# Layer 0 of a two-layer graph network on one core: where TensorE does a node group's values, turns and tables within its step

## The chip, the cores and the metric

The kernel runs on one core of one Trainium2 chip. The metric is the device time of one execution in microseconds (us); the time of a kernel is the median of several executions. Engines are named as in the profile: PE is TensorE, PEld its weight loads, DVE is VectorE, ACT is ScalarE, POOL is GpSimd, SP is SyncE, which here only issues DMAs.

## The reference

A graph of 6250 nodes (128 values each) and 200000 edges, sorted by destination node, passes through two layers, each followed by a residual sum and a layer norm.

```
# layer 0, a transformer convolution
h = x @ Wx.T + bx;  q, k, v = h @ Wq.T + bq, h @ Wk.T + bk, h @ Wv.T + bv
e = concat([msg, cos(|last_update[src] - t| * time_w + time_b)]) @ We.T
alpha = softmax over the edges of one dst of  sum(q[dst] * (k[src] + e)) / sqrt(128)
m = segment_sum((v[src] + e) * alpha, dst)
h = h + tanh(h @ A.T + m + b_ac);   x1 = layernorm(x + tanh(h))
# layer 1, an edge network: relu(concat(x1[src], x1[dst]) @ We1 + be1) @ We2 + be2,
# summed by dst, then a node network, residual and layer norm
```

## The kernel before

Layer 0 works on 196 chunks of 1024 edges (128 partitions by J = 8). Since the edges are sorted by destination, a chunk's destinations lie in a window of W = 80 nodes. The chunks are run by hardware loops: a turn of the loop holds 7 steps (SLOTS), u = 0 to 6, one chunk each, and there are 28 turns. Every engine runs its own list of steps, and the engines meet through semaphores. SLOTS = 7 is also the number of buffers for gathered rows (`he`).

What a step does for the chunks near c, engine by engine:

- POOL, `gather(c)` (L955 to L968): 8 indirect DMAs that fetch the rows of `h_table` for the chunk's sources into `he[u]`. Before them it waits for `sum_full`, that is, for TensorE's sums of the chunk that had this buffer seven chunks ago. TensorE sums chunk c-2 in its step c, so POOL starts the gathers of chunk c+5 when TensorE's sums in step c are reported.
- TensorE, `step(c)` (L1038): `spread_top` of chunk c-1 (L1014, to `p_small`), `turn_top(c)` (L1007), `scores` of c+1 (L989: 24 records of matmuls, as the profile counts them), `turn_back` of c-3 (L1031, 2 records), `sums` of c-2 (L1020, 16 records of 193 columns), and `turn` of c+2 (L971, 12 transposes: 4 for `turn_full[2]` and twice 4 for `turn_full[0]` and `[1]`).
- ACT: `copy_turns` of c+1 (L1131, three copies of `p_turn` to `heT`, in the order 2, 0, 1, each waiting for its `turn_full`), `copy_sums` of c-3 (L1123), then the sine features of c+2, exponentials of c-1, and the widened features of c+2.
- DVE: the phases of c+2, `tops_of_nodes(c)` (L1297, waits for `turn_top`), `diagonals`, `add` of c-4 (L1345), `fades` of c-3, `belows` of c-1, then `others` and `masks` of c+1 (L1281: two halves, each waiting for its half of the scores, and a reduction).

TensorE's `scores` of c+1 wait for ACT's three copies; its `turn_back` waits for `copy_sums` of c-3 and for DVE's `add` of c-4.

The last 13 turns (of 28, in a loop of 12 and one behind it) run `step_grouped` instead. They also take one group of 512 finished nodes (G) each through the end of layer 0 and make layer 1's tables of it. The stages are spread over the steps of a turn:

- u = 0: ACT copies the group's sums out of `acc` (`node_take`).
- u = 1: TensorE's `node_values` (L697, 24 records of matmuls into `p_turn[0]` to `[2]`, `val_full`), then DVE's `node_pre` (L715) behind its own step. The same `p_turn` buffers are wanted by `turn`, so TensorE waits for `pre_done` before `turn`.
- u = 2 to 4: tanh, layer norm (ACT and DVE).
- u = 5: TensorE's `node_turn` (L783, 4 transposes, `x1_full`), ACT's `node_copy_x1` (L789); TensorE waits for `x1T_done` before `turn`.
- u = 6: TensorE's `node_tables` (L796, 8 records of 256 columns, `tables_full`), DVE's `node_copy_rows` (L803) behind its own step; TensorE waits for `rows_done` before `turn`. ACT then stores the two tables.

Layer 1 is not touched: it has loops of its own, from L1684 on.

Of the kernel before, what the change touches and what calls it, by code (L numbers as in the profile page):

```python
# [38 lines left out]
def gnn_kernel(nc, x, src, dst, edge_attr, edge_weight, node_vec, time_w, time_b, Wx, bx, Wq, bq, Wk, bk,  # L39
# [28 lines left out]
    with ExitStack() as whole:  # L68
# [6 lines left out]
        def val(eng, v):  # L75
            return v if isinstance(v, int) else eng.snap(v)

        def again(eng, s, v):

            if not isinstance(v, int) or v > 0:  # L80
                eng.wait_ge(s, v)
# [393 lines left out]
        def shift(c, k):  # L475

            return c[0] + (c[1] + k) // SLOTS, (c[1] + k) % SLOTS
# [4 lines left out]
        def is_last(c):  # L482
            return isinstance(c[0], int) and number(c) == NCH - 1

        def is_first(c):
            return isinstance(c[0], int) and number(c) == 0
# [29 lines left out]
        with ExitStack() as ctx:  # L516
# [316 lines left out]
            def layer0_round(r):  # L833
# [3 lines left out]
                with ExitStack() as c2:  # L837
                    block = c2.enter_context(nc.Block())

                    def count(c):  # L840

                        return (c[0] + base) * SLOTS + c[1]
# [4 lines left out]
                    def prob_of(c):  # L847
                        return probs[third(c)]
# [10 lines left out]
                    def behind(c, k):  # L859

                        return not (isinstance(c[0], int) and number(c) < k)
# [108 lines left out]
                    def _(e):  # L970
                        def turn(c):  # L971

                            u = c[1]
                            n = count(c)
                            n0, n1 = val(e, n), val(e, n + 1)
                            e.wait_ge(he_done, n1)

                            again(e, turn_done[2], n0)
                            for k in range(J // 2):

                                mm = e.transpose(p_turn[2][:, k * P:(k + 1) * P], rest_of(c)[:, k, :, :].rearrange("p f q -> p (f q)"), ident[:, :])  # L981
                            mm.then_inc(turn_full[2], 1)
                            for h in range(2):
                                again(e, turn_done[h], n0)
                                for k in range(4):
                                    mm = e.transpose(p_turn[h][:, k * P:(k + 1) * P], he[u][:, 4 * h + k, A2:WIDE], ident[:, :])  # L986
                                mm.then_inc(turn_full[h], 1)

                        def scores(c):  # L989

                            u = c[1]
                            n = count(c)
                            n0, n1 = val(e, n), val(e, n + 1)
                            e.wait_ge(win_in[u], val(e, (c[0] + base) * 64 + 64))
                            e.wait_ge(turn_done[2], n1)
                            for h in range(2):
                                e.wait_ge(turn_done[h], n1)

                                again(e, masked[h], n0)
                                for k in (0, 2):  # L1000
                                    pair = (4 * h + k) // 2
                                    e.matmul(p_score[h][:, k:k + 2, :], heT2[:, pair * P:(pair + 1) * P], qk_two[u][:, :, :], start=True, stop=False)  # L1002
                                    for j in (4 * h + k, 4 * h + k + 1):
                                        mm = e.matmul(p_score[h][:, j % 4, :], heT1[:, j * P:(j + 1) * P], qk_win[u][:, :], start=False, stop=(j % 2 == 1))  # L1004
                                mm.then_inc(score_full[h], 1)

                        def turn_top(c):  # L1007

                            n = count(c)
                            e.wait_ge(top_j_done, val(e, n + 1))  # L1010
                            again(e, top_n_done, val(e, n))
                            e.transpose(p_topT, top_j[:, :], ident[:, :]).then_inc(topT_full, 1)

                        def spread_top(c):  # L1014

                            e.wait_ge(top_d_done, val(e, count(c) + 1))
                            again(e, level_done, val(e, count(c)))
                            e.matmul(p_tops, ones[0:W + 1, :], top_d[c[1]][:, :, :], start=True, stop=True).then_inc(top_full, 1)

                        def sums(c):  # L1020
                            u = c[1]
                            prob = prob_of(c)
                            n = count(c)
                            e.wait_ge(prob_done, val(e, n + 1))
                            e.wait_ge(wide_done, val(e, n + 1))
                            again(e, sumT_done, val(e, n))
                            for j in range(J):
                                mm = e.matmul(p_sumT, prob[:, j, :], he[u][:, j, 0:WIDE], start=(j == 0), stop=(j == J - 1))  # L1028
                            mm.then_inc(sum_full, 1)

                        def turn_back(c):  # L1031
                            n = count(c)
                            e.wait_ge(sumT_done, val(e, n + 1))
                            again(e, added, val(e, n))
                            e.transpose(p_sum[:, 0, :], sumT[:, A2:WIDE], ident[0:W, 0:W])
                            e.transpose(p_sum[0:A2, 1, :], sumT[:, 0:A2], ident[0:W, 0:W]).then_inc(back_full, 1)

                        def step(c, between=None, before_turn=None):  # L1038
                            if not is_first(c):
                                spread_top(shift(c, -1))  # L1040
                            turn_top(c)
                            if not is_last(c):
                                scores(shift(c, 1))
                            if between:
                                between()
                            if behind(c, 3):
                                turn_back(shift(c, -3))
                            if behind(c, 2):
                                sums(shift(c, -2))
                            if before_turn:  # L1050
                                before_turn()
                            if not is_last(c) and not is_last(shift(c, 1)):
                                turn(shift(c, 2))


                        def step_grouped(c, k):
                            u = c[1]
                            if u == 1:
                                step(c, lambda: node_values(e, k, 0), lambda: e.wait_ge(pre_done, val(e, k + 1)))
                            elif u == 5:  # L1060
                                step(c, lambda: node_turn(e, k, 0), lambda: e.wait_ge(x1T_done, val(e, k + 1)))
                            elif u == 6:
                                step(c, lambda: node_tables(e, k), lambda: e.wait_ge(rows_done, val(e, k + 2)))
                            else:
                                step(c)
# [984 lines left out]
```

## Time and profile before

| | us |
|---|---|
| median of 3 executions (5277.44 to 5301.07) | 5290.53 |
| the profiled execution, its own time | 5293.57 |
| its span in the trace | 5291.5 |
| PE busy / PEld busy | 3353.5 / 3002.7 |
| POOL busy | 3012.9 |
| DVE busy | 2529.0 |
| ACT busy | 1767.2 |
| mean share of TensorE's clock granted | 0.749 |

The span is the trace's first to last instruction; the execution's own time has some 2 us around it. No engine is busy for more than 63% of the span. Layer 0 ends at about 2850 us, and its 13 turns with node groups begin at about 1515 us.

### The profile page before, as it was taken

The numbers are of one execution on the slowest core, as the hardware profiler recorded it, in microseconds if no ns is written. First come the engines' busy times: TensorE is split into PE (matmuls) and PEld (weight loads), VectorE is DVE, ScalarE is ACT, GpSimd is POOL, SyncE is SP. The second block draws the span as 40 slices with busy tenths as digits, with TensorE's granted clock in tenths as the row PEclk, the third lists the DMA queues.
The fourth block names the chain that finished last, engine by engine and source line by source line (L and its number), as shares of the span: only waits on it lengthen the run. The fifth ranks groups of instructions, "written<-read, shape, count | busy, mean of one in ns | idle before, by whom it ended". The sixth has DMA issues, their size and how long they took to land. (4 is left out here: it accounts for less than half of the span.)

```text
span 5291.5 us, 74810 instructions
## 1 busy us (share of the span) xinstructions
PE 3353.5 (63%) x19048; PEld 3002.7 (57%) x19049; DVE 2529.0 (48%) x5599; ACT 1767.2 (33%) x2915; POOL 3012.9 (57%) x3138
## 2 busy tenths in 40 slices
PE   5677777777877777776773444445544565665655
PEld 2676676766766666666662444444444454554545
DVE  2555555555555555555563333433333343434344
ACT  2555555555555555555551101111111111111111
POOL 5356655666555555555542666666666566665663
PEclk7777878788788888888886666666666666666666
DMA  5222222222223222322322222222222232222231
GB/s 152 79 62 63 62 62 62 62 63 63 62 66 81 68 69 71 78 67 70 81 62 74 69 76 75 77 73 77 76 73 75 77 80 76 81 80 76 80 83 49
DMA packets 440134, 387.93 MB, mean 73 GB/s; under 512 B 270569, under 2 KB 365081, under 8 KB 439866
## 3 DMA queue, kind: packets, MB, share of 16 engines
q0 software_dynamic: 100032, 217.87, 16.4%
q1 hardware_dynamic: 312392, 151.94, 11.3%
q10 hardware_dynamic: 27634, 17.29, 1.1%
q8 instruction: 27, 0.44, 0.0%
q14 instruction: 49, 0.39, 0.0%
HBM read 356.77 MB, written 29.97 MB: 73 GB/s over the span
## 5 line engine op out<-in xcount | busy, mean ns | idle before, releaser
L963 POOL DMA_INDIRECT he<-h_table,src_i x1563 | 1516.3, 970 | 1224.1 <-issue 471.2
L1768 POOL DMA_INDIRECT msg<-p_table,src x1563 | 1478.3, 946 | 992.1 <-issue 454.0
L1785 PE MATMUL p_edge<-r_win,hotT 80*128 80x128 f32 x3136 | 572.7, 345 | 738.8 <-DVE msg L1919 446.1
L1785 PEld LDWEIGHTS p_edge<-r_win,hotT 80*128 80x128 f32 x3136 | 514.7, 251 | 795.2 <-issue 495.2
L1796 PE MATMUL p_sumT<-msg,hot 128*80 128x129 f32 x3136 | 585.9, 360 | 371.3 <-ACT sumT L1854 223.5
L1796 PEld LDWEIGHTS p_sumT<-msg,hot 128*80 128x80 f32 x3136 | 535.7, 210 | 413.6 <-issue 383.2
L1846 ACT ACTIVATE msg<-msg 128x1024 f32<-128x1024 f32 x196 | 207.1, 1057 | 1630.8 <-DVE msg L1919 1258.5
L1919 DVE TENSOR_TENSOR msg<-msg,p_edge 128x512 f32<-128x512 f32 x392 | 255.6, 680 | 726.2 <-remote 680.8
L1004 PEld LDWEIGHTS p_score<-qk_win,heT 128*128 128x128 f32 x3136 | 585.9, 250 | 0.0
L1004 PE MATMUL p_score<-qk_win,heT 128*128 128x80 f32 x3136 | 572.9, 318 | 0.0
L1291 DVE SCALAR_TENSOR_TENSOR score<-other,p_score 128x320 f32<-128x320 bf16 x392 | 186.7, 487 | 766.4 <-remote 721.5
L1002 PE MATMUL p_score<-qk_two,heT 128*128 128x160 f32 x1568 | 498.9, 410 | 77.9 <-ACT heT L1140 62.2
L1140 ACT ACTIVATE heT<-p_turn 128x512 f32<-128x512 f32 x588 | 317.7, 595 | 629.2 <-PE p_turn L981 295.2
L1909 DVE SCALAR_TENSOR_TENSOR hotT<-dst_row,start_b,p_iota 80x1024 f32<-80x1024 int32 x196 | 402.6, 2054 | 138.3 <-remote 135.1
L986 PE MATMUL p_turn<-ident,he 128*128 128x128 f32 x1568 | 279.3, 318 | 188.1 <-issue 187.6
L1028 PE MATMUL p_sum<-he,qk 128*80 128x193 f32 x1792 | 365.0, 360 | 34.5 <-issue 34.5
L1002 PEld LDWEIGHTS p_score<-qk_two,heT 128*128 128x128 f32 x1568 | 320.0, 253 | 110.0 <-issue 96.4
L986 PEld LDWEIGHTS p_turn<-ident,he 128*128 128x128 f32 x1568 | 220.7, 164 | 229.6 <-issue 229.2
L1028 PEld LDWEIGHTS p_sum<-he,qk 128*80 128x80 f32 x1792 | 292.3, 169 | 71.4 <-issue 36.7
L1929 DVE TENSOR_TENSOR acc<-acc,p_sum 128x160 f32 x196 | 62.7, 320 | 551.8 <-remote 438.1
L1149 ACT ACT_TABLE_LOAD x167 | 214.3, 1283 | 216.1 <-issue 123.7
L1028 PE MATMUL p_sum<-he,prob 128*80 128x193 f32 x1344 | 251.4, 341 | 21.8 <-issue 21.7
(207 smaller groups left out, 4581.4 us busy)
## 6 DMA issues: line engine op xcount, KB each, us to landing
dst_row<-in_dst_dram SPq DMA_DIRECT2D x196, 320.0 KB
feat<-in_edge_attr_dram SPq DMA_DIRECT2D x196, 128.0 KB
he<-h_table,src_i POOLq DMA_INDIRECT x1563
msg<-p_table,src POOLq DMA_INDIRECT x1563
qk_win<-qk_table SPq DMA_DIRECT2D x196, 40.0 KB
qk_two<-qk_table SPq DMA_DIRECT2D x392, 20.0 KB
r_win<-r_table SPq DMA_DIRECT2D x196, 40.0 KB
qk_table<-qk SPq DMA_DIRECT2D x13, 512.0 KB
```

Source lines behind the costliest of these rows:

```text
L963: e.indirect_dma_start(out=he[u][:, j, 2 * FE:2 * FE + ROW], out_offset=None, in_=h_table[:, :], in_offset=bass.IndirectOffsetOnAxis(ap=sr ...
L986: mm = e.transpose(p_turn[h][:, k * P:(k + 1) * P], he[u][:, 4 * h + k, A2:WIDE], ident[:, :])
L1002: e.matmul(p_score[h][:, k:k + 2, :], heT2[:, pair * P:(pair + 1) * P], qk_two[u][:, :, :], start=True, stop=False)
L1004: mm = e.matmul(p_score[h][:, j % 4, :], heT1[:, j * P:(j + 1) * P], qk_win[u][:, :], start=False, stop=(j % 2 == 1))
L1028: mm = e.matmul(p_sumT, prob[:, j, :], he[u][:, j, 0:WIDE], start=(j == 0), stop=(j == J - 1))
L1140: e.activation(to, p_turn[q][:, :], ACT.Copy).then_inc(turn_done[q], 1)
L1149: e.activation(prob[:, :, :], prob[:, :, :], ACT.Exp).then_inc(prob_done, 1)
L1768: e.indirect_dma_start(out=msg[u][:, j, 0:D], out_offset=None, in_=p_table[:, :], in_offset=bass.IndirectOffsetOnAxis(ap=src_i[u][:, j:j + ...
L1785: mm = e.matmul(p_edge[h][:, j % 4, :], hotT_of(c)[:, j, :], r_win[u][:, :], start=True, stop=True)
L1796: mm = e.matmul(p_sumT[:, :], hot[u][:, j, :], msg[u][:, j, 0:D + 1], start=(j == 0), stop=(j == J - 1))
L1909: e.scalar_tensor_tensor(out=hotT_of(c)[:, :, :], in0=dst_row[u][:, :].rearrange(row_j, j=J), scalar=start_b[0:W, bass.ds(number(c), 1)], ...
L1919: e.tensor_tensor(part, part, p_edge[h][:, :, :], ALU.add).then_inc(both_done[h], 1)
```

## The change

In TensorE's step the node group's piece (`between`: values at u = 1, turns at u = 5, tables at u = 6) stands behind `turn_back` and `sums`, where it stood ahead of them. No instruction is added or removed, the other engines' lists stay as they are, and in the steps without such a piece nothing moves. The waits ahead of `turn` (`before_turn`) stay behind both.

```diff
@@ -1041,12 +1041,13 @@
                             turn_top(c)
                             if not is_last(c):
                                 scores(shift(c, 1))
-                            if between:
-                                between()
                             if behind(c, 3):
                                 turn_back(shift(c, -3))
                             if behind(c, 2):
                                 sums(shift(c, -2))
+
+                            if between:
+                                between()
                             if before_turn:
                                 before_turn()
                             if not is_last(c) and not is_last(shift(c, 1)):
```

## Rows read from the trace of the kernel before

**Rows 1.** The page's costliest groups: busy, mean ns, idle before.

```profile
L963 POOL DMA_INDIRECT he<-h_table,src_i x1563 | 1516.3, 970 | 1224.1 <-issue 471.2
L1140 ACT ACTIVATE heT<-p_turn 128x512 f32<-128x512 f32 x588 | 317.7, 595 | 629.2 <-PE p_turn L981 295.2
```

**Rows 2.** Busy time by stretch: a turn without groups, one with, twelve with.

```profile
1410.49:1502.96 92.47, 73.23 (x400) 66.50 (x399) 51.81 (x134) 50.60 (x85) 54.42 (x56) 0.76 0.27 62
1700.32:1802.53 102.21, 75.66 (x435) 67.67 (x435) 57.54 (x159) 54.71 (x92) 53.67 (x57) 0.82 0.29 71
1529.02:2742.54 1213.52, 871.57 (x5214) 776.67 (x5215) 696.31 (x1903) 658.41 (x1096) 646.52 (x673) 0.85 0.30 72
```

**Rows 3.** Timeline of a plain step, POOL's first gathers: start, us, idle before.

```profile
1502.96 0.95 POOL L963 DMA_INDIRECT he<-h_table,src_i  x1 [3.11 <-remote]
...
1516.04 0.95 POOL L963 DMA_INDIRECT he<-h_table,src_i  x1 [3.03 <-remote]
```

**Rows 4.** Timeline of the same step, TensorE: scores' first, sums.

```profile
1504.17 0.87 PE L1002 MATMUL p_score<-qk_two,heT 128*128 128x160 f32 x2
...
1509.86 2.78 PE L1028 MATMUL p_sum<-he,prob 128*80 128x193 f32 x16
```

**Rows 5.** Timeline of the same step, DVE: the second half of the masks.

```profile
1515.07 0.49 DVE L1291 SCALAR_TENSOR_TENSOR score<-other,p_score 128x320 f32<-128x320 bf16 x1 [4.95 <-remote]
```

**Rows 6.** Timeline of a turn with a group, POOL's first gathers (u = 6, 0, 1, 2, 3).

```profile
1700.32 0.95 POOL L963 DMA_INDIRECT he<-h_table,src_i  x1 [3.14 <-remote]
...
1716.20 0.95 POOL L963 DMA_INDIRECT he<-h_table,src_i  x1 [5.17 <-PE p_sum L1028]
...
1732.54 1.01 POOL L963 DMA_INDIRECT he<-h_table,src_i  x1 [6.63 <-PE p_sum L1028]
...
1750.49 0.95 POOL L963 DMA_INDIRECT he<-h_table,src_i  x1 [8.20 <-PE p_sum L1028]
...
1763.52 0.94 POOL L963 DMA_INDIRECT he<-h_table,src_i  x1 [3.32 <-remote]
```

**Rows 7.** Timeline, TensorE at u = 6: tables, sums, turn.

```profile
1710.36 2.27 PE L799 MATMUL p_turn<-hT 128*128 128x256 f32 x8
...
1712.61 2.78 PE L1028 MATMUL p_sum<-he,prob 128*80 128x193 f32 x16
1716.65 0.63 PE L981 MATMUL p_turn<-ident,rest 128*128 128x128 f32 x4 [1.27 <-DVE hT L808]
```

**Rows 8.** Timeline, TensorE at u = 0: `turn_top`, sums.

```profile
1718.27 0.27 PE L1012 MATMUL p_small<-ident,qk 128*80 128x128 f32 x1
...
1726.43 5.29 PE L1028 MATMUL p_sum<-he,qk 128*80 128x193 f32 x16
```

**Rows 9.** Timeline, DVE: `node_copy_rows` at u = 6, `tops_of_nodes` at u = 0.

```profile
1715.13 1.28 DVE L808 TENSOR_TENSOR hT<-p_turn,hT 128x512 f32<-128x512 f32 x2
...
1725.20 0.29 DVE L1299 TENSOR_REDUCE top_n<-p_small 80x1 f32<-80x128 f32 x1 [6.65 <-remote]
```

**Rows 10.** Timeline, TensorE at u = 1: values, sums, turn.

```profile
1736.52 0.43 PE L710 MATMUL p_turn<-we_bvT,hT 65*128 65x129 f32 x2
...
1741.52 0.27 PE L710 MATMUL p_turn<-we_bvT,hT 65*128 65x129 f32 x1 [2.15 <-issue]
...
1745.26 4.42 PE L1028 MATMUL p_sum<-he,qk 128*80 128x193 f32 x16
1749.52 0.60 PE L981 MATMUL p_turn<-ident,rest 128*128 128x128 f32 x4
```

**Rows 11.** Timeline, DVE at u = 1: masks' second half, `node_pre`.

```profile
1744.50 0.49 DVE L1291 SCALAR_TENSOR_TENSOR score<-other,p_score 128x320 f32<-128x320 bf16 x1 [2.35 <-remote]
...
1746.25 0.21 DVE L722 TENSOR_SCALAR node_s<-p_turn 128x2 f32<-128x2 f32 x2
...
1747.18 1.13 DVE L731 SCALAR_TENSOR_TENSOR hT<-p_turn,node_s,hT 128x128 f32<-128x128 f32 x4
```

**Rows 12.** Timeline of a plain step with late scores: TensorE's sums, POOL's next gather.

```profile
988.08 2.78 PE L1028 MATMUL p_sum<-he,qk 128*80 128x193 f32 x16
...
992.16 0.95 POOL L963 DMA_INDIRECT he<-h_table,src_i  x1 [2.78 <-PE p_sum L1028]
```

## The prediction, made before the result

> **What bounds the kernel now.** I read the page first. No engine is busy for two thirds of the span, so the busy times decide little; the question is what paces a step. Of the costliest groups POOL's gathers stand on top: 970 ns each, with as much as 0.8 us of idle time a gather [rows 1]. I then compared stretches: seven steps without a node group take 92.47 us (13.2 a step); twelve turns with a group take 1213.52 us, 101.1 a turn [rows 2]. The 13 turns that the change touches so cost some 9 us each over a plain turn. That sum, 13 x 8.7 = 113 us, is about all that a better order could give back.
>
> Next the timeline of one plain step, engine by engine. POOL starts its 8 gathers at 1502.96 and the next 8 at 1516.04 [rows 3]. TensorE's scores start at 1504.17 and are over when its sums start, at 1509.86; the sums' records end at 1512.64 [rows 4]. But DVE's second half of the masks, which waits for nothing but the end of those scores, starts at 1515.07 after 4.95 us idle [rows 5], and POOL, which waits for the sums, at 1516.04 after 3.03 us [rows 3]. The reader is to see that what TensorE finishes while gathers run is seen by the others only in one burst, 12.1 us after the first gather was issued. (Gathers are issued for 8 x 1.25 = 10 us of these, so the burst comes some 2 us after the last.) A plain step is thus a ring: gathers 12.1, sums reported with the burst, 0.9 us to POOL's next issue: 13.0. TensorE has finished the sums well before, so it has slack there.
>
> I call G the issue of a step's first gather, and count from it. What TensorE ends before about G+2 is seen at once; what it ends later is held: `turn_top` at G+2.3 (1718.54) was seen at G+9.0 (1725.20 [rows 8, 9]).
>
> **The change, part by part.** Nothing is added or removed; three pieces swap places with 18 records of TensorE (2 of `turn_back`, 16 of sums). No DMA is issued by these pieces, and no queue but TensorE's is reordered. What hangs on the swap: POOL's next gathers (on the sums), and on the other side DVE's `node_pre` and `node_copy_rows` and TensorE's own `turn`, which waits for them.
>
> *u = 6, tables.* Now: the tables stand from 1710.36 for 2.27 us, then the sums end at 1715.39, and POOL issues at 1716.20, 15.9 after its last [rows 6, 7]. After: the sums end 2.3 us sooner, at about 1713.2, and POOL issues at about G+13.8. That sums which start this late still pay nothing more is seen in a plain step: sums that ended at 990.86 released gathers at 992.16 [rows 12]. The tables then end at about 1715.5. DVE began `node_copy_rows` at 1715.13 for 1.28 us [rows 9], right behind its own reduction; that goes 0.5 later. So `turn` starts at about 1717.2, which was G+0.45 of u = 0 (1716.65 [rows 7]) and is now G+3.1, since G itself is 2.1 sooner.
>
> *u = 0, what is late next.* Its length now is 16.34 [rows 6]: `turn_top` is seen at G+9.0, the sums start 1.2 later and take 5.29 [rows 8, 9]. After, `turn` and `turn_top` (15 records) are done inside the held stretch. From both sides: `turn_top` is seen at G+9.0 as now, or with the burst at G+12.1; sums take 2.78 [rows 4] or 5.29 [rows 8], a ratio of 1.9 that I read as TensorE's clock at 2.4 or at 1.2 GHz. Length 9.0+1.2+2.78+0.8 = 13.8 to 12.1+1.2+5.29+0.8 = 19.4. I take the middle, 16.6. u = 6 and 0 together: 13.8+16.6 = 30.4 against 15.9+16.3 = 32.2. The turn shown is 1.1 longer than the mean of twelve [rows 2], of which I put 0.7 here: a gain of 1.1 a turn, between -1.7 and +3.9.
>
> *u = 1, values.* Now: scores, then 24 records of values, which TensorE starts at 1736.52 and cannot go on with after some 18 (1741.52, idle 2.15 before); then the burst at 1744.50, the rest, and the sums only from 1745.26, for 4.42; POOL issues at 1750.49, 17.95 after its last [rows 6, 10, 11]. After: turn back and sums are the 18 records that get in before the stop, as in each plain step; they are reported with the burst, and POOL issues at about 1745.5, G+13.0: 5.0 us sooner. The values are now what is stopped. 20 of their records are left at 1744.5. Sums of 193 columns take 0.17 [rows 4] to 0.33 us a record [rows 8], so these of 128 take 0.12 to 0.22: 2.4 to 4.4 us. They end at 1746.9 to 1748.9, which is G+1.4 to G+3.4 of the new stretch of gathers, on the edge of where reports are held. `node_pre` takes 2.06 us (1746.25 to 1748.31 [rows 11]). With a prompt report `turn` starts at about 1749.0 to 1751.0, G+3.5 to 5.5; with one held to G+7, at G+9. Now it starts at 1749.52, just before POOL's issue.
>
> *u = 2, what is late next.* Now 13.03 [rows 6]. After, ACT's three copies of the turned rows (0.6 us each [rows 1]) wait for reports from inside the held stretch, and behind them in ACT's queue `copy_sums`, behind TensorE's turn the scores and the sums. If nothing were held: `turn` to G+6.6, the copies and the scores at the upper clock to G+10.6, the sums to G+13.6, 14.4 in all. If all is held to the burst: 12.1 + 1.6 of copies + 5.0 of scores (5.7 from 1504.17 to 1509.86 [rows 4], the first half of which can start ahead of the last copy) + 2.8 of sums + 0.8 = 22.3. If the first two copies get through and half of the scores: 19.1. Since `turn` lies deeper in the held stretch than at u = 0, I take a value nearer the upper two, 20.4. u = 1 and 2 together: 13.0+20.4 = 33.4 against 17.95+13.03 = 31.0: a loss of 2.4, between a loss of 4.3 and a gain of 3.6.
>
> *u = 5, turns.* Four transposes go behind the sums, all still before the burst; `x1_full` comes after 18 records instead of before: a loss of 0.3, between 0 and 0.6. The waits ahead of `turn` are hidden in no step, as now.
>
> **The sum.** Per turn +1.1 - 2.4 - 0.3 = -1.6; by 13 turns, 21 us slower. On the profiled execution's 5293.6 (its span of 5291.5 and 2.1 around it) that is 5314.6; it stands 3.0 over the median, so 5312 as a median. Layer 1 keeps its time.
>
> Two rules of the skill bear on this. The Trainium skill, "PSUM — Partial Sum Buffer", section "Engine vs sequencer instructions", says that an increment attached to a matmul fires when the instruction completes. The trace disagrees as far as others see it: 5.2 us lie between the end of the scores and DVE's start [rows 4, 5]. By that rule the first rival below would be the result. The same skill, "TensorE: Matmul & The Clock Gate", section on the array's 32x32 sub-arrays, gives TensorE a queue of 64 instructions, weight loads counted. The stop after 24 scores and 18 values, each with its load, is 84 instructions, so by that rule 20 had been reported by then; it changes nothing in the sum.
>
> **Rivals.**
> - *Both handovers are early and nothing is held (faster).* POOL gets the sums sooner and turns inside the gathers are seen promptly. For it: the 5.0 and 2.1 us at POOL are read off directly. Against it: the held reports [rows 5, 9]. u = 0 then takes 13.8 and u = 2 14.4: per turn 3.9+3.6-0.3 = 7.2, 94 us: 5197. Half of it, when reports are held for a few us only, gives 5244. It decides from the point where `turn`'s reports at u = 2 are seen before about G+8.
> - *All is held (much slower).* u = 0 19.4 and u = 2 22.3: per turn 1.7+4.3+0.3 = 6.3, 82 us: 5373. For it: `turn_top` waited 6.65 us in a milder case [rows 9]. Against it: TensorE could add a record at 1741.52, 3 us ahead of the burst [rows 10], so some reports do get through, and the first two copies need only 8 transposes.
> - *A swap of waits (no change).* What POOL wins at u = 1 and 6 is lost at u = 2 and 0: 5290. That is my sum with u = 2 at 18.8 instead of 20.4.
>
> **How the numbers follow.** A difference of 0.5% (26 us) is about what a measurement of this kernel can tell from none. Chances: my forecast (net loss of 0.6 to 3.5 a turn, 5298 to 5336) 0.40, all or nearly all held 0.16, swap 0.20, early handover in part 0.14, in full 0.10. The likeliest one's own range is 5298 to 5336. The range for 8 in 10 goes from 5230 to 5380, since cases of both signs hold much of the chance. Over half of the forecast's 0.40 lies above 5317, and with all held that makes slower 0.38; faster takes the early cases, 0.24; the same is left with 0.38.
>
> **What would show it right or wrong.** In the changed kernel's timeline POOL's gathers at u = 1 should come 13.0 after those before (now 17.95), and at u = 6 about 13.8 (now 15.9). The next stretch, u = 2, should grow from 13.0 to about 20, with ACT's copies (L1140) as what waits, and u = 0 should stay at 16 to 17. TensorE's idle time before L981 at u = 1 should name DVE's L731 and be 2 us or more. If u = 2 stays under 17 I am wrong on the holding, and the kernel is faster; if POOL still starts late at u = 1, then on what the sums wait for.

## The result and the profile after

| | before | after |
|---|---|---|
| median, us | 5291.68 (6 executions) | 5346.98 (6 executions) |
| ratio of the times, 95% interval | | 1.0104 [1.0088, 1.0121] |
| the profiled execution / its span, us | 5293.57 / 5291.5 | 5344.36 / 5342.0 |
| twelve turns with a group, us | 1213.5 [rows 2] | 1261.3 |
| mean share of TensorE's clock granted | 0.749 | 0.739 |

The change makes the kernel 55 us slower, 1.0%. I had forecast 21 us slower. One of after's six executions took 11889.91 us and is left out; the others lie between 5334.93 and 5360.21.

The page of the changed kernel, costliest groups (busy, mean ns, idle before). The gathers' instruction is no slower than in [rows 1]; what grew is the idle time around it and around ACT's copies (629.2 to 708.9 us):

```profile
L963 POOL DMA_INDIRECT he<-h_table,src_i x1563 | 1509.9, 966 | 1278.2 <-issue 471.7
...
L1141 ACT ACTIVATE heT<-p_turn 128x512 f32<-128x512 f32 x588 | 318.7, 596 | 708.9 <-issue 278.7
```

Busy time by stretch in the changed kernel: a turn without groups, one with, twelve with. These answer to [rows 2]. The first two windows are rounded. From first gather to first gather the turn without groups is as long as it was, 92.4 us (1410.58 to 1503.02) against 92.47. The turn with a group is 102.9 us long (1703.89 to 1806.75), 2.2 less than its window and less than the mean of twelve, 105.1. All of the loss lies in the turns with a group, and in them POOL and TensorE have the same instructions as before:

```profile
1410.00:1503.00 93.00, 75.20 (x405) 67.89 (x402) 52.20 (x135) 51.35 (x86) 54.32 (x56) 0.74 0.27 62
1703.90:1809.00 105.10, 74.98 (x444) 67.82 (x445) 59.41 (x163) 57.00 (x94) 54.86 (x58) 0.84 0.29 71
1529.10:2790.40 1261.30, 917.36 (x5215) 829.42 (x5216) 697.48 (x1903) 656.56 (x1094) 643.88 (x672) 0.81 0.29 69
```

TensorE's granted clock in the twelve turns fell from 0.85 to 0.81, and its busy time rose from 871.6 to 917.4 us. That is a rival of its own for the loss. In the two steps that will be seen to grow, its sums are no longer than before, though: 4.4 us for 5.3 at u = 0 and 3.5 for 4.2 at u = 2, means of twelve turns. What the lower clock costs in the scores and turns was not separated.

The timeline of one such turn, POOL's first gathers at u = 6, 0, 1, 2 and 3. It answers to [rows 6]: the starts now lie 13.99, 16.30, 13.06 and 20.43 us apart, where they lay 15.88, 16.34, 17.95 and 13.03 apart:

```profile
1703.89 0.94 POOL L963 DMA_INDIRECT he<-h_table,src_i  x1 [3.31 <-remote]
...
1717.88 0.94 POOL L963 DMA_INDIRECT he<-h_table,src_i  x1 [3.31 <-PE p_sum L1028]
...
1734.18 0.94 POOL L963 DMA_INDIRECT he<-h_table,src_i  x1 [6.63 <-PE p_sum L1028]
...
1747.24 0.94 POOL L963 DMA_INDIRECT he<-h_table,src_i  x1 [3.37 <-PE p_sum L1028]
...
1767.67 0.94 POOL L963 DMA_INDIRECT he<-h_table,src_i  x1 [10.75 <-PE p_sum L1028]
```

Over twelve turns, the mean distances of these same rows are:

| us from first gather to first gather | u = 6 | 0 | 1 | 2 | 3, 4, 5 each | turn |
|---|---|---|---|---|---|---|
| before | 15.55 | 15.49 | 17.38 | 13.62 | 12.9 to 13.1 | 101.1 |
| after | 14.45 | 18.11 | 13.06 | 20.41 | 13.0 to 13.1 | 105.1 |
| difference | -1.10 | +2.62 | -4.32 | +6.79 | 0 | +4.0 |

So the early handovers are there (u = 6 and 1), and each is paid back with more in the step behind it (u = 0 and 2). Of the 55 us, 13 x 4.0 = 52 are this.

TensorE in that turn, u = 6 and the start of u = 0; it answers to [rows 7]. The sums cannot all be issued ahead of the burst of reports (12 go, then two stops of 0.47 and 1.84 us), so the tables come behind the burst, and `turn` stands at G+3.7 of the next gathers, where it stood at G+0.45:

```profile
1711.65 2.12 PE L1028 MATMUL p_sum<-he,prob 128*80 128x193 f32 x12
1714.25 0.32 PE L1028 MATMUL p_sum<-he,prob 128*80 128x193 f32 x1 [0.47 <-issue]
1716.42 0.65 PE L1028 MATMUL p_sum<-he,prob 128*80 128x193 f32 x3 [1.84 <-issue]
1716.91 2.97 PE L799 MATMUL p_turn<-hT 128*128 128x256 f32 x8
1721.60 0.66 PE L981 MATMUL p_turn<-ident,rest 128*128 128x128 f32 x2 [1.72 <-issue]
...
1724.56 0.28 PE L1012 MATMUL p_small<-ident,qk 128*80 128x128 f32 x1
```

DVE from u = 6 to u = 2: `node_copy_rows`, `tops_of_nodes` of u = 0, masks and `node_pre` of u = 1, `tops_of_nodes` of u = 2; it answers to [rows 9, 11]. `turn_top` ended at 1724.84 and DVE, idle for 5.99 us, saw it at 1729.49. That is G+11.6; before it was seen at G+9.0:

```profile
1720.07 1.29 DVE L808 TENSOR_TENSOR hT<-p_turn,hT 128x512 f32<-128x512 f32 x2 [1.23 <-issue]
...
1729.49 0.29 DVE L1300 TENSOR_REDUCE top_n<-p_small 80x1 f32<-80x128 f32 x1 [5.99 <-remote]
...
1746.19 0.89 DVE L1292 SCALAR_TENSOR_TENSOR score<-other,p_score 128x320 f32<-128x320 bf16 x2 [5.02 <-remote]
...
1749.10 0.23 DVE L722 TENSOR_SCALAR node_s<-p_turn 128x2 f32<-128x2 f32 x2 [0.67 <-issue]
...
1750.04 1.13 DVE L731 SCALAR_TENSOR_TENSOR hT<-p_turn,node_s,hT 128x128 f32<-128x128 f32 x4
...
1759.09 0.29 DVE L1300 TENSOR_REDUCE top_n<-p_small 80x1 f32<-80x128 f32 x1 [5.94 <-remote]
```

TensorE at u = 1 and 2; it answers to [rows 10]. The sums are over before the burst, as in a plain step. The values run from 1745.33 to 1748.91, `turn` at 1751.41 is G+4.2, half of the scores get through, and the other half waits 3.37 us for ACT. The 2.50 us ahead of `turn` are put down to "issue", but end 0.24 us behind DVE's `node_pre` (L731 above, 1750.04 and 1.13 long):

```profile
1742.43 2.78 PE L1028 MATMUL p_sum<-he,qk 128*80 128x193 f32 x16
1745.33 0.27 PE L710 MATMUL p_turn<-we_bvT,hT 65*128 65x129 f32 x1
...
1748.52 0.39 PE L712 MATMUL p_turn<-aT,hT 128*128 128x128 f32 x2
1751.41 0.84 PE L981 MATMUL p_turn<-ident,rest 128*128 128x128 f32 x4 [2.50 <-issue]
...
1759.73 0.90 PE L1002 MATMUL p_score<-qk_two,heT 128*128 128x160 f32 x2 [3.37 <-ACT heT L1141]
...
1762.85 4.01 PE L1028 MATMUL p_sum<-he,prob 128*80 128x193 f32 x16
```

ACT's second and third copy of that step: the third waits 5.27 us, and starts with the same burst as DVE above (1759.08 and 1759.09, G+11.8):

```profile
1753.21 0.60 ACT L1141 ACTIVATE heT<-p_turn 128x512 f32<-128x512 f32 x1 [0.26 <-issue]
1759.08 0.60 ACT L1141 ACTIVATE heT<-p_turn 128x512 f32<-128x512 f32 x1 [5.27 <-remote]
```

The view of waits over the twelve turns (waiter, what it waited for: us in total, times, longest). First before:

```profile
POOL he L963 <- PE p_sum L1028: 258.8, 45, 8.9
...
POOL he L963 <- remote: 123.0, 40, 3.4
...
DVE top_n L1299 <- remote: 54.8, 10, 6.7
```

and after:

```profile
POOL he L963 <- PE p_sum L1028: 282.6, 39, 13.0
...
DVE top_n L1300 <- remote: 147.4, 26, 7.5
...
POOL he L963 <- remote: 140.3, 45, 3.4
```

POOL's waits grew by 23.8 + 17.3 = 41 us, where the twelve turns grew by 48. DVE's wait for `turn_top`, which stands inside the stretch of gathers, grew from 54.8 to 147.4 us.

### The profile page after: what moved, and what is told of

It is laid out like the page before. It is cut to its first block and busy times, and to the rows that moved or that the text cites. A ratio compares the mean times of both kernels' runs of the same rounds, so it can differ in the third digit from the quotient of the medians.

```text
span 5342.0 us, 74810 instructions
## 1 busy us (share of the span) xinstructions
PE 3409.0 (64%) x19048; PEld 3063.2 (57%) x19049; DVE 2530.8 (47%) x5599; ACT 1765.7 (33%) x2915; POOL 3002.7 (56%) x3138
## 5 line engine op out<-in xcount | busy, mean ns | idle before, releaser
L1004 PEld LDWEIGHTS p_score<-qk_win,heT 128*128 128x128 f32 x3136 | 611.5, 260 | 0.0
L1004 PE MATMUL p_score<-qk_win,heT 128*128 128x80 f32 x3136 | 595.9, 328 | 0.0
L1002 PE MATMUL p_score<-qk_two,heT 128*128 128x160 f32 x1568 | 515.5, 422 | 115.6 <-ACT heT L1141 85.2
L1141 ACT ACTIVATE heT<-p_turn 128x512 f32<-128x512 f32 x588 | 318.7, 596 | 708.9 <-issue 278.7
L986 PE MATMUL p_turn<-ident,he 128*128 128x128 f32 x1568 | 278.1, 319 | 175.0 <-issue 174.5
L1028 PE MATMUL p_sum<-he,qk 128*80 128x193 f32 x1792 | 362.3, 360 | 22.7 <-issue 22.6
L986 PEld LDWEIGHTS p_turn<-ident,he 128*128 128x128 f32 x1568 | 223.4, 165 | 212.9 <-issue 212.7
L1028 PE MATMUL p_sum<-he,prob 128*80 128x193 f32 x1344 | 262.7, 351 | 20.2 <-issue 19.9
```

Source lines behind the costliest of these rows:

```text
L1141: e.activation(to, p_turn[q][:, :], ACT.Copy).then_inc(turn_done[q], 1)
```

## The experiments

The theory to be tested has two parts. **Part one, what is lost**: behind the sums, the values and the tables are late for `node_pre` and `node_copy_rows`, and with them the next `turn`, whose successors (ACT's copies, the scores, the sums) then end later than POOL's next gathers can use. **Part two, why it costs so much**: what TensorE ends inside the stretch of gathers is seen only in the burst. The rivals: the turns or the x1 copy do it; it is POOL's handover and not TensorE's chain; the order is a gain as soon as nothing is held. A part of the loss by the lower granted clock was not tested by an edit.

Something must be said first of the chips. The runs fell on chips of two kinds. Where before and after were first measured, and in the two runs e9b (values and tables) and e6b (ACT's copy of x1), the kernel before takes 5291 us. In all other runs the same kernel before takes 4111 to 4116 us. I call them the slow and the quick chip. Each run is compared with the kernel before on its own chip.

**The kernel before, again** (no edit).

> The kernel before, unchanged, for its trace on the chip of the last four runs, where it took 4114 us and not 5290. Two theories of the difference. (a) On that chip TensorE's reports are not held while gathers run, so a plain step is POOL's own 8 x 1.25 = 10.0 us and not 13.1: every stretch of a group's turn should be 10.0 to 11 us, and TensorE's ends should be seen at once. (b) The chip is faster as a whole: then single instructions (970 ns a gather, 680 ns a 128x512 sum on DVE) are shorter too. If this run falls on a chip like the first one, it takes about 5290 again and shows stretches of 13.0 us.

Measured: 4115.99 us in one execution (median of the kernel before beside it: 4111.05). On the quick chip POOL issues gathers back to back, 10.0 us a plain step, 71.2 us a turn with a group. It is the bound of a plain step; in a turn with a group its own 56 x 1.25 = 70.0 us and TensorE's chain (71.0, measured below) lie close together. Its timeline:

```profile
1177.36 0.94 POOL L963 DMA_INDIRECT he<-h_table,src_i  x1 [0.30 <-issue]
1178.61 0.94 POOL L963 DMA_INDIRECT he<-h_table,src_i  x1 [0.30 <-issue]
```

The gather itself takes nearly what it takes on the slow chip, 0.94 us for 0.95 [rows 3], and plain sums 2.78 [rows 4]. ACT's copies take 593 ns for 595, DVE's masks 485 for 487. TensorE's matmuls are somewhat shorter in the mean (the turns, L986, 273 ns for 318) at a granted clock of 0.815 for 0.749. In layer 0 the difference lies mostly in the waits between engines.

**The changed kernel, again** (the change, nothing else).

> The changed kernel, unchanged. Where reports are held: 5345, ratio 1.010. Where they are not, the values alone cost 31 us and the tables alone 11, so about 42 us: 4156, ratio 1.010, with the loss at u = 2 (12 us or more for 10) and the rest at u = 0. If the order's loss came only from held reports, the ratio would be 1.000 there.

Measured: 4216.75 us against 4111.05, ratio 1.025 [1.0232, 1.0267]. The cost is 106 us here, twice that on the slow chip and more than twice the 42 us that I expected of this chip. By POOL's first gathers u = 2 takes 13.3 us for 10.2, and u = 6, 0 and 1 take 11.4, 11.9 and 11.7 for 10.0, 10.1 and 10.8. The twelve turns, first before, then after:

```profile
1164.80:2018.60 853.80, 750.62 (x5186) 699.24 (x5184) 688.62 (x1894) 644.79 (x1088) 638.62 (x672) 0.93 0.42 103
```

```profile
1161.10:2102.80 941.70, 764.94 (x5174) 707.48 (x5173) 684.25 (x1878) 639.22 (x1077) 636.43 (x672) 0.92 0.38 93
```

That is 87.9 us more, and the view of waits gives all of it to one line. Before:

```profile
POOL he L963 <- issue: 197.5, 645, 1.2
POOL he L963 <- PE p_sum L1028: 17.7, 27, 1.8
```

After, with what TensorE's `turn` (L981) waits for:

```profile
POOL he L963 <- issue: 195.6, 623, 1.3
POOL he L963 <- PE p_sum L1028: 107.5, 49, 4.7
...
PE p_turn L981 <- DVE hT L731: 30.1, 12, 2.5
...
PE p_turn L981 <- DVE hT L808: 20.7, 12, 1.7
...
PE p_turn L981 <- ACT hT L794: 13.5, 12, 1.1
```

In the kernel before on this chip TensorE is not once idle ahead of L981 in these turns. The three new waits, for `node_pre`, `node_copy_rows` and the copy of x1, are there in each of the twelve and make 5.4 us a turn. By its sums TensorE's turn grew by 7.8 us, from 71.3 to 79.0; where the other 2.4 us arise I have not traced.

In the changed kernel's timeline on the quick chip, TensorE stands idle ahead of `turn` behind values and behind tables, and names DVE's `node_pre` and `node_copy_rows`. `turn_top` ends at 1169.57, with POOL in the middle of its gathers, and DVE starts on it 0.04 us later:

```profile
1163.64 0.39 PE L712 MATMUL p_turn<-aT,hT 128*128 128x128 f32 x2
1166.54 0.63 PE L981 MATMUL p_turn<-ident,rest 128*128 128x128 f32 x4 [2.51 <-DVE hT L731]
...
1169.15 0.42 PE L1012 MATMUL p_small<-ident,qk 128*80 128x128 f32 x1
...
1215.30 1.89 PE L799 MATMUL p_turn<-hT 128*128 128x256 f32 x8
1218.91 0.63 PE L981 MATMUL p_turn<-ident,rest 128*128 128x128 f32 x4 [1.72 <-DVE hT L808]
```

```profile
1169.61 0.29 DVE L1300 TENSOR_REDUCE top_n<-p_small 80x1 f32<-80x128 f32 x1 [1.34 <-PE p_small L1012]
```

So this report is not held on the quick chip, and the change still loses. The rival by which prompt reports make it a gain falls, and part two of the theory is not needed for a loss.

**One piece alone.** Each moves one piece behind the sums and leaves the others ahead of them:

```diff
-                                step(c, lambda: node_values(e, k, 0), lambda: e.wait_ge(pre_done, val(e, k + 1)))
+                                step(c, None, lambda: e.wait_ge(pre_done, val(e, k + 1)), lambda: node_values(e, k, 0))
...
-                                step(c, lambda: node_turn(e, k, 0), lambda: e.wait_ge(x1T_done, val(e, k + 1)))
+                                step(c, None, lambda: e.wait_ge(x1T_done, val(e, k + 1)), lambda: node_turn(e, k, 0))
...
-                                step(c, lambda: node_tables(e, k), lambda: e.wait_ge(rows_done, val(e, k + 2)))
+                                step(c, None, lambda: e.wait_ge(rows_done, val(e, k + 2)), lambda: node_tables(e, k))
```

where `step` calls its new last argument, `behind_sums`, behind `sums` and ahead of `before_turn`.

Values: 

> Only the values (u = 1) stand behind the sums; turns and tables stay ahead of them. Held-report theory (what TensorE completes while a step's gathers run is seen by the others only some 12 us after the first gather was issued): POOL's stretch at u = 1 falls from 17.4 to 13.0 us and the one at u = 2 grows from 13.6 to 20.4, as in the changed kernel, u = 6 and u = 0 stay at 15.6 and 15.5. Net +2.5 us a turn, 13 turns: 32 us slower, about 5324, ratio 1.006. Rival (the loss is only TensorE's exposed wait for node_pre, whatever POOL does): the time is lost in the step with the values itself, so u = 1 stays long at 17 us or more and u = 2 stays near 13 to 14.

Tables: 

> Only the tables (u = 6) stand behind the sums. Held-report theory: POOL's stretch at u = 6 falls from 15.6 to about 14.4, the one at u = 0 grows from 15.5 to about 18.1, u = 1 and u = 2 stay at 17.4 and 13.6. Net +1.5 us a turn, 20 us slower, about 5311, ratio 1.004. With the values alone (+32 us) this adds up to the change's 52 to 55 us. Rival (exposed wait alone): u = 6 grows, u = 0 stays.

Turns: 

> Only the turns (u = 5, four transposes) stand behind the sums. On the chip where the last runs were made (4111 us before; reports are seen at once) the values alone cost 31 to 33 us, the tables alone 11 to 15, all three 104. What is left, 55 to 60 us, is what I expect of the turns alone: ratio 1.014, from ScalarE, which sits in its queue with its copy of x1 ahead of the step's exponentials. Rival: the pieces are not additive, because POOL's own 70 us a turn hides the first few us of each, and all three together come out of that cover; then the turns alone cost 10 to 30 us (ratio 1.002 to 1.007). On a chip where reports are held (5290 us before): x1 is reported in the same burst either way, 0 to 4 us, ratio 1.000.

Values and tables: 

> The values and the tables behind turn back and sums, the turns still ahead of them. Where the kernel before takes 4111 to 4116 us: values alone cost 31 to 33 us, tables alone 11 to 15, turns alone 27, all three together 104. If the losses simply add up, this takes 42 to 48 us more than before, some 4155 to 4162. If POOL's 70.1 us of gathers a turn cover a part of each loss while it stands alone, a part that is used up once, the last one added costs its full price and this one lies further up: between 4165 and 4190 (104 less 27 would be 77, so 4190 at most). Where the kernel before takes 5290 us instead: the loss of the whole change there, 55 us, less at most 5 for the turns, so 5340 to 5347; the POOL stretch at u = 2 is then 20 us and that at u = 1 13 us.

| behind the sums | chip | median | before | more, us | ratio [95%] |
|---|---|---|---|---|---|
| values | quick | 4146.79 | 4113.61 | 33 | 1.0075 [1.0061, 1.0088] |
| tables | quick | 4128.78 | 4113.61 | 15 | 1.0026 [1.0009, 1.0044] |
| turns | quick | 4140.59 | 4113.95 | 27 | 1.0064 [1.005, 1.0078] |
| all three | quick | 4216.75 | 4111.05 | 106 | 1.025 [1.0232, 1.0267] |
| values, tables | slow | 5333.05 | 5290.87 | 42 | 1.0085 [1.0068, 1.0102] |
| all three | slow | 5346.98 | 5291.68 | 55 | 1.0104 [1.0088, 1.0121] |

On the quick chip each piece alone costs time by the medians. The first two expectations had been made for the slow chip. That the values' 33 us meet the 32 expected is luck, since on the quick chip the reason given there, held reports, is absent. For the turns I had expected 55 to 60 us and measured 27, the rival's case. In their run ACT waits 42.6 us over the twelve turns for the turned x1, where it waited 16.2, and TensorE 13.5 us for ACT's copy, where it waited for none.

The tables' 15 us are the weakest of these. The execution of theirs that was traced took 4113.39 us, no more than the kernel before, though `turn` waited 20.7 us for `node_copy_rows` in it. The three of its eight executions at a granted clock of 0.821 or more took 4107 to 4119 us, and the five at 0.814 to 0.817 took 4128 to 4137. So an exposed wait ahead of `turn` can be absorbed, and the clock has a part in this row.

The three together cost 31 us more than their sum of 75. As I read it, the room between two bounds accounts for this, in part at least. By TensorE's sums a turn of the kernel before takes 71.3 us, POOL's issue bounds it at 70.0, and buffers gathered seven steps ahead let TensorE be late in one step and catch up in the next. One delay a turn is partly absorbed, three are not. POOL's wait for the sums over the twelve turns, one traced execution each, is 17.7 us before, 19.9 with the tables, 43.5 with the values, 54.4 with the turns and 107.5 with all.

On the slow chip values and tables alone bring 42 of the 55 us, and the step distances are nearly those of the whole change: 14.28, 18.62, 13.03 and 19.48 us at u = 6, 0, 1 and 2. The run took 5333 us; I had expected 5340 to 5347. Its POOL in one turn (u = 1 and 2 start here, 13.03 and 19.55 us):

```profile
1727.55 0.94 POOL L963 DMA_INDIRECT he<-h_table,src_i  x1 [8.48 <-PE p_sum L1028]
...
1740.58 0.94 POOL L963 DMA_INDIRECT he<-h_table,src_i  x1 [3.20 <-remote]
...
1760.13 0.94 POOL L963 DMA_INDIRECT he<-h_table,src_i  x1 [9.88 <-PE p_sum L1028]
```

**Half of the gathers.** In layer 0 only four of eight gathers of each step are issued (but for the first turn), with the semaphore counts to match. The rows of j = 0 to 3 are left out, so the output is not the reference's, and the runs serve for their times only. It was run in the order of before, with the change on top, and in the order of before once more.

```diff
-                            for j in range(SKIP if is_last(c) else 0, J):
+                            for j in range(SKIP if is_last(c) else 0 if at_zero else J // 2, J):
```

The order of before: 

> The kernel before, but from its second turn on layer 0 gathers only the rows of j = 4 to 7, 4 gathers a step for 8; the rows of j = 0 to 3 stay those of an older chunk. Held-report theory: the burst of reports comes 4 x 1.25 + 2.1 = 7.1 us after the first gather, so the ring of a plain step is 8.0 us, and what binds is TensorE's and DVE's own work, some 10 to 11 us a plain step for 13.1. About 180 steps save 2 to 3 us each: 4750 to 4930 us. Rival (TensorE's reports are late for a reason of its own, its queue or its clock, and gathers do not matter): plain steps stay at 13 us.

The order of after: 

> The changed kernel with the same half of the gathers (j = 0 to 3 not gathered from the second turn on). Held-report theory: reports of a turn done inside the stretch are held to 7.1 us and not to 12.1, so u = 2 and u = 0 lose up to 5 us less each than in the changed kernel; against the kernel before with half the gathers the order costs between -15 and +15 us, where with all gathers it costs 52. Rival (exposed waits alone): the same 50 us or so as with all gathers.

The order of before, once more: 

> The kernel before with only half of the gathers (the columns j = 0 to 3 of each step are not gathered; the output is therefore not the reference's). It is the run that tells whether the gathers hold TensorE's reports, where the kernel before takes 5290 us: there the burst comes 12.1 us after a step's first gather, some 2 us after the last of 8. If it follows the gathers, it comes about 2 us behind the last of 4, at 4 x 1.25 + 2 = 7.0 us, and a plain step takes either 7.0 + 1.0 = 8.0 us or what TensorE itself needs with nothing held, 8.3 us (as measured where the kernel before takes 4111 to 4116 us); the whole comes near 4000 to 4300 us. If the burst has a time of its own, whatever POOL does, a plain step stays at 13.1 us and the whole above 5200 us. Where the kernel before takes 4111 to 4116 us, this repeats 3941 us.

Measured, all on the quick chip, one execution each: 3941.33 us, 4058.85 us, and 3947.24 us. With POOL out of the way a plain step falls to TensorE's own 8.33 us. The pair says what the order is worth to TensorE's chain when POOL does not pace it: 117.5 us, 9.0 a turn (by TensorE's sums a turn takes 71.0 and 79.7 us). TensorE's idle time ahead of `turn` is nil in the first and 2.5, 1.7 and 1.1 us at u = 1, 6 and 5 in the second, 5.4 us of these 8.7. I had expected between -15 and +15 for that pair, and this was the clearest miss of the study: I had put the loss down to the holding of reports alone, and the loss is there without it. The third run was meant for the slow chip, where it would have told whether the burst follows the gathers. It fell on the quick one and only repeats the first.

**POOL's gathers held back.** The change, and on top POOL waits at u = 4 and 6 of its own list for `turn` before it gathers, so that `turn` is never inside a stretch of gathers.

```diff
+                            if k is not None and u in (4, 6):
+                                e.wait_ge(turn_full[1], val(e, count(c) - 2))
+                                e.sem_inc(passed, 1)
```

> The changed kernel, in which POOL, in the steps with values and tables, starts the next gathers only when TensorE's turn of that step is reported. Where reports are held (held-report theory): u = 1 grows from 13.1 to 18 or 19, u = 2 falls from 20.4 to 13.0 to 13.5; u = 6 grows from 14.4 to 18, u = 0 falls from 18.1 to 13.5: some 2 to 3 us a turn faster than the changed kernel, 5305 to 5320. Rival (the exposed waits alone lose the time): POOL's wait comes on top, 5380 or more. Where reports are not held POOL is the bound and its wait costs in full: about 5 us at each of two steps, up to 130 us slower than the changed kernel.

Measured on the quick chip: 4214.57 us against 4111.05, 1.0245 [1.0226, 1.0264], the same as the change alone. I had expected up to 130 us more there, a miss. The wait moves POOL's idle time (from first gather to first gather now 16.5 us at u = 1 and 12.9 at u = 6, with 10.2 and 10.1 at u = 0 and 2) and does not add to the whole: where TensorE's chain is the bound, POOL may wait elsewhere for nothing. Whether this edit mends the slow chip's loss was not measured there.

**Two tries at a better kernel.** In the first, the tables stand behind the sums (as above), DVE copies the rows ahead of its masks, and ACT copies x1 behind its step:

```diff
-                            elif u == 5:
-                                step(c, lambda: node_copy_x1(e, k))
...
+                            if u == 5:
+                                node_copy_x1(e, k)
...
-                            elif u == 6:
-                                node_copy_rows(e, k)
...
+                            step(c, (lambda: node_copy_rows(e, k)) if u == 6 else None)
```

> A version that tries to win: values stay ahead of the sums, tables go behind them, DVE copies the tables' rows ahead of its masks instead of behind them, and ACT copies the turned x1 behind its exponentials. Where reports are held: u = 6 13.5 to 14.5 (before 15.6), u = 0 13.5 to 15.5 (before 15.5), the rest as before: 1 to 2 us a turn, 5265 to 5280. Where they are not held, stretches are POOL's 10.0 us already and little is left: within 10 us of before.

Measured on the quick chip: 4131.91 us against 4111.05, 1.0048 [1.0033, 1.0063]. It is no better than the tables alone (15 us more than before), and 21 us more where I had expected at most 10.

In the second, only ACT's copy of x1 is moved, as in the first four lines of this diff:

> The kernel before with one edit on ScalarE: at u = 5 it copies the node group's x1 after its step (turned rows, exponentials, sums) and not between. This is the handover that the turns behind the sums made later, tried from the other side. Where the kernel before takes 4111 to 4116 us: if the copy ahead of the exponentials delays the step, the step at u = 5 (11.6 us between TensorE's sums, against 7.7 to 9.1 of a plain one) gets shorter by up to 0.6 us, and the kernel by 0 to 8 us, since POOL's 70.1 us a turn are then the bound: 4103 to 4113. If TensorE's turns of u = 5 wait for that copy instead, it gets longer by about 1 us a turn, 13 us: 4127. Where the kernel before takes 5290 us, no change within 10 us, since the handovers all lie before the burst.

Measured on the slow chip: 5284.14 us against 5290.87, 0.999 [0.9978, 1.0001]: no change that can be told, as expected there. Its steps at u = 1 are longer (18.6 us) and those at u = 0 and 2 shorter (15.1 and 13.2), 101.5 us a turn for 101.1 before. No version beat the kernel before.

## Why the prediction was right, and where it was off

The sign, and on the slow chip the course of the steps, were right; the size was short, 21 us forecast against 55 measured. 5347 is inside the wide range of 5230 to 5380. It is outside the range of the likeliest case, 5298 to 5336, and lies between that and the rival by which all is held (5373). Step by step:

- *u = 1, POOL issues 13.0 after its last*: 13.06. The gain forecast as 5.0 us was 4.3 as a mean, since the kernel before stood at 17.38 in the mean and not at the example's 17.95.
- *u = 2 grows to 20.4 with ACT's copies as what waits*: 20.41, between 17.3 and 22.7 in single turns. I had picked 20.4 between two worked cases, 19.1 and 22.3, without a row for it; that it meets the mean so closely is luck. u = 1 and 2 together lost 2.5, forecast 2.4. `turn` was forecast at G+3.5 to 5.5 with a prompt report, and lies at 5.3 in the mean. The idle time ahead of it is 2.5 us, as the signs to look for had said.
- *u = 6 at G+13.8*: 13.99 in the turn shown, 14.45 in the mean. I had the tables end at G+15.2; the last sums wait for the burst, and they end at 1719.88, G+16.0. `turn` came out at G+3.7 instead of G+3.1.
- *u = 0, the step that failed.* I took 16.6, the middle between `turn_top` seen at G+9.0 with sums at the upper clock, and seen with the burst with sums at the lower. Measured 18.11 in the mean of twelve turns: `turn_top` seen at G+11.7, the sums 1.2 later, 4.4 for them, 0.8 to POOL. The report is with the burst in eleven turns of twelve (10.3 in the other); so the row of before, where `turn` stood at G+0.5, was no guide for one at G+2.6 or later. The middle was right only for the sums (4.4 between 2.78 and 5.29). u = 6 and 0 together lost 1.5 a turn where I had a gain of 1.1: 2.6 x 13 = 34 us, which is about the whole gap between 21 and 55.
- *u = 5, a loss of 0.3*: 0.03 in POOL's distance there. On the slow chip the turns' part of the whole would be the difference between two runs, 55 - 42 = 13 us, some 1 a turn. The intervals of the two ratios overlap, so it is not shown. The traces differ at u = 2 (20.41 against 19.48) and the other way at u = 0 (18.11 against 18.62), not at u = 5. How the turns would cost time there I have not found. The prediction has the waits ahead of `turn` "hidden in no step, as now". On the quick chip the kernel before hid all of them, and on the slow one nearly all at u = 1 (0.3 us of idle time in the mean, 2.5 after), but not at u = 6 (1.2, after 1.7).
- *The rivals.* That nothing would be held and the kernel 94 us faster was priced as if the prompt chain was free of loss. The quick chip is that rival's own case and gives 106 us slower. What I left out there: the sums (2.9 us with `turn_back`) had been the cover for `node_pre` and `node_copy_rows`. With them ahead of the piece, TensorE stands idle 2.5 and 1.7 us ahead of `turn`, and the chain of TensorE, ACT and TensorE again starts later by that; nothing in it was waiting for earlier sums, since POOL had seven buffers.

What is shown: that moving the values and the tables makes most of the loss on the slow chip, and each piece some on the quick one, the tables least surely; that on the quick chip the loss is POOL waiting for TensorE's sums, with new waits ahead of `turn` that make 5.4 of the 7.8 us by which TensorE's turn grew; and that in the slow chip's trace the successors start together with the burst. How the 55 us of the slow chip divide between the later `turn`, the holding and the clock is not measured.

What stays open: whether it is the gathers that hold the reports. The burst comes about 12.1 us behind the first of a step's 8 gathers, and so some 3.3 us behind the start of the last (7 x 1.25 = 8.8), but no run with fewer gathers fell on a chip that holds them. The trace of before on the slow chip speaks for it. In layer 0 it has two stretches in which TensorE works and POOL issues no gather, from 122.5 to 174.0 us and from 2760.7 us on, behind the last gather. In these, DVE and ACT start on TensorE's turns, scores and `turn_top` at most 0.8 us after they could, in all 49 cases. The last gather, and `turn_top` 35 us behind it, which DVE sees 0.05 us after its end:

```profile
2758.42 0.95 POOL L963 DMA_INDIRECT he<-h_table,src_i  x1 [0.31 <-issue]
```

```profile
2793.82 0.27 PE L1012 MATMUL p_small<-ident,qk 128*80 128x128 f32 x1
```

```profile
2794.14 0.29 DVE L1299 TENSOR_REDUCE top_n<-p_small 80x1 f32<-80x128 f32 x1 [0.97 <-PE p_small L1012]
```

It is a coincidence in time and no experiment: other work is missing from these stretches too.

The Trainium skill, "PSUM — Partial Sum Buffer", section "Engine vs sequencer instructions", has an increment fire when its matmul completes. On the quick chip the trace agrees: 0.04 us from the end of `turn_top` to DVE's start. On the slow chip it does not, as far as DVE sees it: 4.65 us for the same pair of lines (1724.84 to 1729.49). Whether the increment or its arrival is late the trace does not tell.

## What to carry to other kernels

Before a producer is moved behind other work, see what that other work covered: here 2.9 us of `turn_back` and sums hid the wait for another engine's copy, and they hid it only while they stood between the two. An earlier handover to an engine that has seven buffers in hand buys nothing unless that engine's wait is the end of the chain. And when a cost is known from a row at one place, ask whether it holds 2 us further on: in the turn read for the forecast `turn_top` was seen ahead of the burst, at G+9.0, and with `turn` some 2 us later it was seen with the burst.

## What was not expected of the hardware

The same kernel takes 5291 us on one chip and 4111 to 4116 on another, with 0.94 to 0.95 us a gather and 2.78 us for plain sums on both. In layer 0 the most visible difference is when TensorE's completed work is seen by the others: within 0.04 us where I read it on the quick chip, and up to the burst, some 12 us after a step's first gather, on the slow one. A plain step of 13.1 us there is 10.0 here. Layer 0's last sums end at 2812.6 us on the slow chip and at 2083.0 on the quick one, 730 us of the 1177 between the two traced spans; the rest lies in layer 1, which I did not read. An order of work tuned on one of them is judged by other waits on the other; the change is a loss on both, 1.0% and 2.5%.
